# Row maxima and their scales on VectorE instead of TensorE for five of eight blocks, and input work spread over more steps

## The chip, the cores and the metric

The kernel runs on one core of one Trainium2 chip. The metric is the device time of one execution in microseconds (us), as the median of several executions; less is better. TensorE (PE in the profile) does the matrix products, its weight loads are listed as PEld. VectorE (DVE) and ScalarE (ACT) do the element-wise work, GpSimd (POOL) prepares weights early on, and the queue of SyncE (SP) issues the transfers.

## What is computed

```python
def act_quant(x):
    scale = 127.0 / jnp.clip(jnp.max(jnp.abs(x), axis=-1, keepdims=True), 1e-05, None)
    return jnp.clip(jnp.round(x * scale), -128.0, 127.0) / scale

scale = cond @ norm_w.T + 1.0
ms = jnp.mean(x * x, axis=-1, keepdims=True)
h = x * (scale[:, None, :] * jax.lax.rsqrt(ms + EPS))
u = h @ up_w.T
val, gate = jnp.split(u, 2, axis=-1)
h = val * jax.nn.gelu(gate, approximate=False)
hq = act_quant(h)                 # straight-through form left out
wq = weight_quant(down_w)         # to -1, 0, 1 times one scale
y = hq @ wq.T
return y + x
```

x is 4 x 1024 x 512 in float32, the hidden width is 2048, so up_w has 4096 rows. What matters here is act_quant: every token needs the largest absolute value of its 2048 hidden values before any of them can be rounded.

## The kernel before

The 4096 tokens are worked on in NB = 8 blocks of 512, numbered from 0 (the third block is b = 2). Within a block the hidden width is cut into J = 16 steps of 128, so that step n = 16 b + j makes hidden tile j of block b. A hidden tile has the 128 hidden values on the partitions and the 512 tokens along the free axis. Each float32 product is made of three float16 products (high and low parts of x and of the weights, names x_hi, x_lo, w_hi, w_lo). From block 2 on the value and gate products of a step are made of seven half-sized ones in place of eight (in_seven); for that the inputs of each block are first combined into sums and differences: difference on VectorE into ta, tb and xt, high on ScalarE (cast to x_hi), low on VectorE (the rest, x_lo). This is the "input work" of block b + 1, and it is done during block b, in steps 2, 3 and 15. It needs norm(b + 1, ...), four VectorE instructions in step 1.

There is no scheduler: each engine runs a program written out by hand, and semaphores hold it where it needs another. In a step n from block 2 on TensorE runs first_pair(n), third(n-1), gates(n-1), second(n), fourth(n-1), together 42 matmuls of 256 columns. ScalarE runs copies(n), absolute(n-2), gelu(n-1), and then the input work. VectorE runs hidden(n-2) (L1105), second_val(n-1) (L1093, waits for third), peak_of(n-2) (L1118, L1115 in step 0 of a block: the running maximum h_max over hidden tiles), residual (L1161), scaled (L1140: tiles of the block before are multiplied by their scale, which lies in ps_m), seed_gate(n) (L1088, waits for second(n) and is waited for by third(n)), rounded (L1147), then norm and the input work. From step 3 on two, one and one tiles of the block before are scaled and rounded per step, in turn (Q_COUNT), so steps 3, 6, 9 and 12 have two.

After these products TensorE has a tail in some steps. In steps 15, 0, 1 and 2 it is the second product, down, of an earlier block (16 matmuls of 512 columns, L674). The row maxima need TensorE too. h_max holds one maximum per partition and token; turn_max(b-1) at the end of step 1 of block b turns its four 128 x 128 parts by a transpose each (L657) into the PSUM bank ps_m. At the head of step 2 VectorE reduces ps_m along the free axis to one maximum per token (row_scales: L1122, L1125, L1127, L1129), with the tokens on the partitions. The scales are needed along the free axis again, equal on all partitions: spread_scale(b-1) in step 2 does that by four more transposes of a broadcast column (L663), ahead of down. norm reads ps_m as well, for the spread row factors of x, up to block 4; from block 5 on these come by a transfer. Once in blocks 3, 4 and 5, in step 11, VectorE runs rsqrt (L1031 to L1045), twelve small instructions. The last block's maxima are turned and spread after the loop.

Of the kernel before, what the change touches and what calls it, by code (L numbers as in the profile page):

```python
# [6 lines left out]
P = 128  # L7
ALU = mybir.AluOpType
ACT = mybir.ActivationFunctionType
F32 = mybir.dt.float32  # L10
# [32 lines left out]
def bass_cond_norm_geglu_bitlinear(  # L43
# [84 lines left out]

    def h_home(b, j):
        return J + j if j < 2 and b % 2 == 1 else j  # L130

    with ExitStack() as ctx:
# [48 lines left out]

        cond_sb = p5[:, 0, 0:B]
# [12 lines left out]
        row_max = sb("row_max", [P, TT], F32)  # L195
        row_rec = sb("row_rec", [P, TT], F32)
        row_scale = sb("row_scale", [P, TT], F32)
        dequant = sb("dequant", [P, 2, TT], F32)
        d_sums = sb("d_sums", [P, ND], F32)
# [82 lines left out]
        row_step = sem("row_step")  # L282
        scale_ready = sem("scale_ready")
# [9 lines left out]
        RS_STEPS = 11  # L293

# [68 lines left out]
        def _(sp):  # L363
# [111 lines left out]
            for n in range(NJ):  # L475
# [41 lines left out]
                if b == NB - 1 and j in (4, 5, 6):  # L517
                    if j == 4:
                        sp.wait_ge(x_lo_ready, made_before(NB))
                    load_late(2 * (j - 4))  # L520
                    load_late(2 * (j - 4) + 1)
# [16 lines left out]
        def _(pe):  # L538
# [121 lines left out]
            def spread_scale(b):  # L660
                pe.wait_ge(scale_ready, b + 1)
# [29 lines left out]
            for n in range(NJ + 1):  # L691
# [22 lines left out]
                if 1 <= b and j == 2:  # L714
                    spread_scale(b - 1)
# [43 lines left out]
        def _(act):  # L759
# [99 lines left out]
            for n in range(NJ + 2):  # L859
# [123 lines left out]
        def _(dve):  # L983
# [77 lines left out]
            def difference(c, k):  # L1061
                before = (c - 2) * 4
                if k == XT1:
                    dve.wait_ge(xn_ready, c * KT + 2)
                    dve.tensor_tensor(ta[:], xt[:, 0:2, HB:TB], xt[:, 0:2, 0:HB], ALU.subtract).then_inc(t_ready, 1)
                elif k == XT2:
                    dve.wait_ge(xn_ready, c * KT + 4)
                    dve.wait_ge(t_ready, before + 1)
                    dve.tensor_tensor(tb[:], xt[:, 2:4, HB:TB], ta[:], ALU.subtract).then_inc(t_ready, 1)
# [49 lines left out]

            def row_scales(b):  # L1120
                dve.wait_ge(max_rows, b + 1)
                dve.tensor_reduce(row_max[:], ps_m[:].rearrange("p (i n) -> p i n", i=TT), AX.X,  # L1122
                                  ALU.max).then_inc(row_step, 1)
                dve.wait_ge(row_step, 3 * b + 1)
                dve.tensor_scalar(row_max[:], row_max[:], CLIP, None, ALU.max).then_inc(row_step, 1)  # L1125
                dve.wait_ge(row_step, 3 * b + 2)
                dve.reciprocal(row_rec[:], row_max[:]).then_inc(row_step, 1)  # L1127
                dve.wait_ge(row_step, 3 * b + 3)
                dve.tensor_scalar(row_scale[:], row_rec[:], QMAX, None, ALU.mult).then_inc(scale_ready, 1)  # L1129

            def row_dequant(b):
                if b == 0:
                    dve.wait_ge(d_step, 5)
                dve.tensor_scalar(dequant[:, b % 2, :], row_max[:], 1.0 / QMAX, d_mean[:], ALU.mult,
                                  ALU.mult).then_inc(dequant_ready, 1)
# [14 lines left out]
            def residual(b, i, bank):  # L1150
# [3 lines left out]
                dve.wait_ge(dequant_ready, b + 1)  # L1154
# [39 lines left out]
            for n in range(NJ + 2):  # L1194
                b, j = divmod(n, J)
                if 1 <= b < NB and j == 2:
# [35 lines left out]
                if n < NJ and in_seven(n):  # L1232
                    seed_gate(n)
                for t in tiles:
# [96 lines left out]
```

## Time and profile before

| | us |
|---|---|
| median of 3 runs | 757.35 (757.11 to 757.44) |
| the profiled execution, device time | 756.66 |
| its span in the profile | 754.9 |
| TensorE busy (matmul) | 735.1, 97% |
| VectorE busy | 545.8, 72% |
| ScalarE busy | 348.7, 46% |
| GpSimd busy | 98.6, 13% |

The profile is of one execution; its span leaves out 1.8 us of the device time (756.66 less 754.9). Matmuls overlap in the rows: one has a duration, and the next starts before it ends, so that what a matmul costs its queue is the distance between two starts.

### The profile page before, as it was taken

The numbers are of one execution on the slowest core, as the hardware profiler recorded it, in microseconds if no ns is written. First come the engines' busy times: TensorE is split into PE (matmuls) and PEld (weight loads), VectorE is DVE, ScalarE is ACT, GpSimd is POOL, SyncE is SP. The second block draws the span as 40 slices with busy tenths as digits, with TensorE's granted clock in tenths as the row PEclk, the third lists the DMA queues.
The fourth block names the chain that finished last, engine by engine and source line by source line (L and its number), as shares of the span: only waits on it lengthen the run. The fifth ranks groups of instructions, "written<-read, shape, count | busy, mean of one in ns | idle before, by whom it ended". The sixth has DMA issues, their size and how long they took to land.

```text
span 754.9 us, 14213 instructions
## 1 busy us (share of the span) xinstructions
PE 735.1 (97%) x5462; PEld 536.5 (71%) x5462; DVE 545.8 (72%) x1066; ACT 348.7 (46%) x677; POOL 98.6 (13%) x137
## 2 busy tenths in 40 slices
PE   3999999999999999999999999999999999999998
PEld 2544444444677887888778887788778887688864
DVE  5467777888689775878667775777758776377747
ACT  5788866443164532553335543444425442243425
POOL 2211376763314000000000000000000000000000
PEclk9999999999999999999999999999999999999999
DMA  8777574756646454343533444343443333453302
GB/s 326 271 270 236 181 270 134 227 183 215 203 135 184 155 159 142 116 141 99 197 118 119 131 128 162 112 159 113 141 160 103 99 98 120 126 171 99 103 29 83
DMA packets 44787, 117.32 MB, mean 155 GB/s; under 512 B 5424, under 2 KB 5680, under 8 KB 43568
## 3 DMA queue, kind: packets, MB, share of 16 engines
q1 hardware_dynamic: 44720, 116.42, 47.8%
q8 instruction: 43, 0.70, 0.4%
q14 instruction: 24, 0.20, 0.1%
HBM read 99.62 MB, written 16.78 MB: 154 GB/s over the span
## 4 chain that ended last, share of the span: by engine, by line
PE 77%; DVE 12%; issue 5%; ACT 4%; DMA 1%; DVEq 0%; SPq 0%; POOL 0%; ACTq 0%
PE ps_v L552 13%; PE ps_v L553 13%; PE ps_v L554 13%; PE ps_y L674 12%; PE ps_g L553 5%; PE ps_g L552 5%; PE ps_g L554 5%; DVE h L1105 2%; DVE h L1140 2%; ACT g L781 2%; DVE h_max L1118 2%; PE ps_v L738 1%; PE ps_v L570 1%; PE ps_g L570 1%; PE ps_g L572 1%
## 5 line engine op out<-in xcount | busy, mean ns | idle before, releaser
L552 PE MATMUL ps_v<-x_hi,w_hi 128*128 128x256 f16 x968 | 264.5, 273 | 3.5 <-DVE ps_g L1088 1.3
L554 PE MATMUL ps_v<-x_hi,w_lo 128*128 128x256 f16 x968 | 264.4, 273 | 0.0
L553 PE MATMUL ps_v<-x_lo,w_hi 128*128 128x256 f16 x968 | 264.4, 273 | 0.0
L763 ACT COPY ps_g<-ps_v 128x256 f32<-128x256 f32 x96 | 34.3, 357 | 226.3 <-PE ps_v L554 226.3
L774 ACT ACTIVATE g<-ps_g,w_unscale 128x512 f32<-128x512 f32 x128 | 87.3, 682 | 67.8 <-PE ps_g L554 67.6
L1093 DVE TENSOR_TENSOR ps_v<-ps_v,p 128x256 f32<-128x256 f32 x96 | 41.4, 431 | 102.0 <-PE ps_v L554 102.0
L781 ACT ACTIVATE g<-h 128x512 f32<-128x512 f32 x128 | 81.3, 635 | 62.1 <-DVE h L1105 61.2
L1118 DVE TENSOR_TENSOR h_max<-g,h_max 128x512 f32<-128x512 f32 x120 | 84.9, 707 | 33.7 <-ACT g L781 25.6
L552 PEld LDWEIGHTS ps_v<-x_hi,w_hi 128*128 128x128 f16 x968 | 94.8, 98 | 19.3 <-DVE ps_g L1088 2.7
L552 PE MATMUL ps_g<-x_hi,w_hi 128*128 128x256 f16 x392 | 107.4, 274 | 0.0
L553 PE MATMUL ps_g<-x_lo,w_hi 128*128 128x256 f16 x392 | 107.4, 274 | 0.0
L554 PE MATMUL ps_g<-x_hi,w_lo 128*128 128x256 f16 x392 | 107.4, 274 | 0.0
L553 PEld LDWEIGHTS ps_v<-x_lo,w_hi 128*128 128x128 f16 x968 | 94.9, 98 | 13.1
L554 PEld LDWEIGHTS ps_v<-x_hi,w_lo 128*128 128x128 f16 x968 | 94.9, 98 | 11.1
L674 PE MATMUL ps_y<-dw,q 128*128 128x512 bf16 x448 | 101.3, 379 | 0.0
L1105 DVE SCALAR_TENSOR_TENSOR h<-ps_v,w_unscale,g 128x512 f32<-128x512 f32 x128 | 95.5, 746 | 2.4 <-PE ps_v L554 2.4
L1140 DVE TENSOR_TENSOR h<-h,ps_m 128x512 f32<-128x512 f32 x128 | 84.1, 680 | 1.8 <-PE ps_m L663 1.8
L674 PEld LDWEIGHTS ps_y<-dw,q 128*128 128x128 bf16 x448 | 43.8, 98 | 47.0
L1088 DVE TENSOR_TENSOR ps_g<-ps_v,p 128x256 f32<-128x256 f32 x96 | 41.3, 430 | 10.1 <-PE ps_v L554 4.3
L570 PE MATMUL ps_v<-x_hi,w_hi 128*128 128x512 f16 x124 | 47.0, 379 | 0.5 <-DVE h L1105 0.5
L1147 DVE TENSOR_SCALAR q<-h 128x512 bf16<-128x512 f32 x112 | 46.9, 440 | 0.3
L570 PE MATMUL ps_g<-x_hi,w_hi 128*128 128x512 f16 x124 | 47.0, 379 | 0.0
(127 smaller groups left out, 910.6 us busy)
## 6 DMA issues: line engine op xcount, KB each, us to landing
w_lo<-w_lo_dram SPq DMA_DIRECT2D x96, 448.0 KB, 3.3
q<-in_up_t_dram SPq DMA_DIRECT2D x16, 512.0 KB, 4.3
xt<-in_x_cols_dram SPq DMA_DIRECT2D x8, 1024.0 KB, 5.3
res<-in_x_rows_dram SPq DMA_DIRECT2D x26, 256.0 KB, 3.6
out_dram<-res SPq DMA_DIRECT2D x26, 256.0 KB, 2.7
sums<-in_up_t_dram SPq DMA_DIRECT2D x12, 512.0 KB, 4.5
xs<-in_x_rows_dram SPq DMA_DIRECT2D x22, 256.0 KB, 3.6
w_lo_dram<-w_lo SPq DMA_DIRECT2D x16, 256.0 KB, 4.3
```

Source lines behind the costliest of these rows:

```text
L552: pe.matmul(to, w_hi[:, wh:wh + P], hi, start=start and kt == 0, stop=False, skip_group_check=True)
L553: pe.matmul(to, w_hi[:, wh:wh + P], lo, start=False, stop=False, skip_group_check=True)
L554: last = pe.matmul(to, w_lo[:, wl:wl + P], hi, start=False, stop=(kt == 1), skip_group_check=True)
L570: pe.matmul(bank, w_hi[:, wh:wh + P], hi, start=start and kt == 0, stop=False)
L674: last = pe.matmul(ps_y[:, i % 2, :], q[:, j * TB + i * P:j * TB + (i + 1) * P], dw[:, j * D:(j + 1) * D], start=(j == 0), stop=(j == J - 1))
L774: act.activation(g[:, n % 3, :], ps_g[:, n % NG, :], ACT.Gelu, scale=w_unscale[:, n % J:n % J + 1]).then_inc(g_ready, 1)
L781: act.activation(g[:, n % 3, :], h[:, at:at + TB], ACT.Abs).then_inc(h_abs_ready, 1)
L1093: dve.tensor_tensor(ps_v[:, n % NV, HB:TB], ps_v[:, n % NV, 0:HB], p5[:, sevens(n) % 2, :], ALU.add).then_inc(v2_ready, 1)
L1105: dve.scalar_tensor_tensor(out=h[:, at:at + TB], in0=ps_v[:, n % NV, :], scalar=w_unscale[:, j:j + 1], in1=g[:, n % 3, :], op0=ALU.mult, o ...
L1118: dve.tensor_tensor(h_max[:], g[:, n % 3, :], h_max[:], ALU.max).then_inc(h_max_ready, 1)
L1140: dve.tensor_tensor(h[:, at:at + TB], h[:, at:at + TB], ps_m[:], ALU.mult).then_inc(scaled_ready, 1)
L1147: dve.tensor_scalar(to[:, j * TB:(j + 1) * TB], h[:, at:at + TB], ROUND, ROUND, ALU.add, ALU.subtract).then_inc(q_ready, 1)
```

## The change

For blocks 2 to 6 (by_vector) the two sets of transposes on TensorE are left out, and VectorE does both. turn_peaks, at the end of step 1 behind the four norm instructions, turns h_max in blocks of 32 x 32 by one transpose of 128 x 512 and reduces each run of 32, which leaves for every token four partial maxima in the four groups of 32 partitions. spread_peaks, in step 2 behind seed_gate, copies three groups to the partitions of the first, reduces the four, does the clip, reciprocal and factor on 32 x 16 elements, copies the result to the three other groups, and fills ps_m by a second transpose of 128 x 512 whose input is broadcast. row_scales is no longer run for these blocks. The one instruction for dequant becomes four on 32 partitions each. Where spread_scale is kept, it stands behind down in step 2 and no longer ahead of it (blocks 0 and 1; only block 1 has a down there). The two other input changes are for the inputs of blocks 4 to 7, made during blocks 3 to 6: of the six VectorE instructions of step 2 only the first difference stays there, two go to step 4, two to step 7 and one to step 10; of ScalarE's seven casts (four in step 2 and three in step 3) two stay in step 2, and one goes to step 5, one to 8, two to 9 and one to 11. New buffers are views of ta and tb; SyncE's late loads into them have one wait more.

```diff
+        turned = ta[:].rearrange("p a n -> p (a n)")
+        peak_rows = tb[:, 0, 0:TB // Q * TT].rearrange("p (k t) -> p k t", k=TT)
+        row_inv = tb[0:Q, 1, 0:TB // Q]
+        scale_all = tb[:, 1, TB // Q:2 * (TB // Q)]
...
+        row_peak = sb("row_peak", [P, TB // Q], F32)
...
+        def by_vector(b):
+            return V_FIRST <= b < NB - 1
...
+                        sp.wait_ge(scale_rows, NB - 1)
...
-                if 1 <= b and j == 2:
-                    spread_scale(b - 1)
                 for c in range(1, RS_DRAM):
                     if n == spread_rs_at(c):
                         spread_rs(c)
                 if b >= 2 and j < 3:
                     down(b - 2, j + 1)
+                if 1 <= b and j == 2 and not by_vector(b - 1):
+                    spread_scale(b - 1)
                 if b >= 1 and j == J - 1:
                     down(b - 1, 0)
-                if 1 <= b and j == 1:
+                if 1 <= b and j == 1 and not by_vector(b - 1):
                     turn_max(b - 1)
...
                         high(b + 1, XT1)
+                    if j == (2 if b < 3 else 5):
                         high(b + 1, XT2)
+                    if j == (2 if b < 3 else 8):
                         high(b + 1, XT3)
-                    if j == 3:
+                    if j == (3 if b < 3 else 9):
                         high(b + 1, XB21)
                         high(b + 1, XB22)
+                    if j == (3 if b < 3 else 11):
                         high(b + 1, XN4)
...
+                    if by_vector(c - 2):
+                        dve.wait_ge(peak_step, (c - 2 - V_FIRST) * PEAK_STEPS + 1)
...
+            def turn_peaks(b):
+
+                dve.wait_ge(h_max_ready, (b + 1) * J)
+                dve.wait_ge(x_hi_ready, made_before(b + 1))
+                dve.wait_ge(x_lo_ready, made_before(b + 1))
+                dve.transpose(turned, h_max[:]).then_inc(max_rows, 1)
+                dve.wait_ge(max_rows, b + 1)
+                dve.tensor_reduce(peak_rows[:, 0, :], turned.rearrange("p (t n) -> p t n", n=Q), AX.X,
+                                  ALU.max).then_inc(peak_step, 1)
+
+            def spread_peaks(b):
+
+                base = (b - V_FIRST) * PEAK_STEPS
+                dve.wait_ge(peak_step, base + 1)
+                for k in range(1, TT):
+                    dve.tensor_copy(peak_rows[0:Q, k, :], peak_rows[k * Q:(k + 1) * Q, 0, :]).then_inc(peak_step, 1)
+                dve.wait_ge(peak_step, base + 4)
+                dve.wait_ge(dequant_ready, dequants(b - 1))
+                dve.tensor_reduce(row_peak[0:Q, :], peak_rows[0:Q].rearrange("p k t -> p t k"), AX.X,
+                                  ALU.max).then_inc(peak_step, 1)
+                dve.wait_ge(peak_step, base + 5)
+                dve.tensor_scalar(row_peak[0:Q, :], row_peak[0:Q, :], CLIP, None, ALU.max).then_inc(peak_step, 1)
+                dve.wait_ge(peak_step, base + 6)
+                dve.reciprocal(row_inv, row_peak[0:Q, :]).then_inc(peak_step, 1)
+                dve.wait_ge(peak_step, base + 7)
+                dve.wait_ge(scale_rows, b)
+                dve.tensor_scalar(scale_all[0:Q, :], row_inv, QMAX, None, ALU.mult).then_inc(peak_step, 1)
+                dve.wait_ge(peak_step, base + 8)
+                for k in range(1, TT):
+                    dve.tensor_copy(scale_all[k * Q:(k + 1) * Q, :], scale_all[0:Q, :]).then_inc(peak_step, 1)
+                dve.wait_ge(peak_step, base + 11)
+                dve.wait_ge(xn_ready, min(b + 3, NB) * KT)
+                dve.wait_ge(scaled_ready, b * J)
+                dve.transpose(ps_m[:], scale_all.unsqueeze(2).to_broadcast([P, TB // Q, Q])).then_inc(scale_rows, 1)
...
+                else:
+                    for k in range(TT):
+                        dve.tensor_scalar(dequant[k * Q:(k + 1) * Q, b % 2, :],
+                                          row_peak[0:Q, :].rearrange("p (i k) -> p k i", k=TT)[:, k, :], 1.0 / QMAX,
+                                          d_mean[0:Q, :], ALU.mult, ALU.mult).then_inc(dequant_ready, 1)
...
-                if 1 <= b < NB and j == 2:
+                if 1 <= b < NB and j == 2 and not by_vector(b - 1):
                     row_scales(b - 1)
...
+                if 1 <= b < NB and j == 2 and by_vector(b - 1):
+                    spread_peaks(b - 1)
...
+                if 1 <= b < NB and j == 1 and by_vector(b - 1):
+                    turn_peaks(b - 1)
+                if 1 <= b < NB - 1:
                     if j == 2:
                         difference(b + 1, XT1)
+                    if j == (2 if b < 3 else 4):
                         difference(b + 1, XT2)
                         low(b + 1, XB11)
+                    if j == (2 if b < 3 else 7):
                         difference(b + 1, XT3)
                         low(b + 1, XT1)
+                    if j == (2 if b < 3 else 10):
                         difference(b + 1, XN4)
```

The new order is shown in block 3 at the turn from step 1 to 2, in step 2, and in step 4. The names are those of the section on the kernel; line numbers of the changed kernel differ.

TensorE, end of step 1 to the head of step 2, before:

```order
L554 MATMUL ps_v<-x_hi,w_lo 128x256
L674 MATMUL ps_y<-dw,q 128x512 x16
L657 MATMUL ps_m<-ident,h_max 128x128 x4
L552 MATMUL ps_v<-x_hi,w_hi 128x256
L553 MATMUL ps_v<-x_lo,w_hi 128x256
```

and after:

```order
L584 MATMUL ps_v<-x_hi,w_lo 128x256
L704 MATMUL ps_y<-dw,q 128x512 x16
L582 MATMUL ps_v<-x_hi,w_hi 128x256
L583 MATMUL ps_v<-x_lo,w_hi 128x256
L584 MATMUL ps_v<-x_hi,w_lo 128x256
```

The four transposes of h_max behind down are gone, and the products of step 2 follow at once.

TensorE, step 2, from its last product to step 3, before:

```order
L554 MATMUL ps_v<-x_hi,w_lo 128x256
L663 MATMUL ps_m<-ident,row_scale 128x128 x4
L674 MATMUL ps_y<-dw,q 128x512 x16
L552 MATMUL ps_v<-x_hi,w_hi 128x256
L553 MATMUL ps_v<-x_lo,w_hi 128x256
```

and after:

```order
L584 MATMUL ps_v<-x_hi,w_lo 128x256
L704 MATMUL ps_y<-dw,q 128x512 x16
L582 MATMUL ps_v<-x_hi,w_hi 128x256
L583 MATMUL ps_v<-x_lo,w_hi 128x256
L584 MATMUL ps_v<-x_hi,w_lo 128x256
```

The four transposes of row_scale ahead of down are gone too.

VectorE, end of step 1, from seed_gate on, before:

```order
L1088 TENSOR_TENSOR ps_g<-ps_v,p 128x256
L1058 SCALAR_TENSOR_TENSOR xt<-xt,cs,ps_m 128x512 x4
L1122 TENSOR_REDUCE row_max<-ps_m 128x4
L1125 TENSOR_SCALAR row_max<-row_max 128x4
L1127 RECIPROCAL row_rec<-row_max 128x4
L1129 TENSOR_SCALAR row_scale<-row_rec 128x4
L1105 SCALAR_TENSOR_TENSOR h<-ps_v,w_unscale,g 128x512
L1093 TENSOR_TENSOR ps_v<-ps_v,p 128x256
```

and after:

```order
L1125 TENSOR_TENSOR ps_g<-ps_v,p 128x256
L1091 SCALAR_TENSOR_TENSOR xt<-xt,cs,ps_m 128x512 x4
L1162 STREAM_TRANSPOSE ta<-h_max 128x512
L1164 TENSOR_REDUCE tb<-ta 128x16
L1142 SCALAR_TENSOR_TENSOR h<-ps_v,w_unscale,g 128x512
L1130 TENSOR_TENSOR ps_v<-ps_v,p 128x256
```

The reduction of ps_m and three small instructions ahead of hidden are replaced by a transpose and a reduction of SBUF data, with nothing of TensorE's between norm and them.

VectorE, step 2, from residual to hidden of step 3, before:

```order
L1161 SCALAR_TENSOR_TENSOR res<-ps_y,dequant,res 128x512
L1088 TENSOR_TENSOR ps_g<-ps_v,p 128x256
L1065 TENSOR_TENSOR ta<-xt 128x512
L1069 TENSOR_TENSOR tb<-xt,ta 128x512
L1083 TENSOR_TENSOR x_lo<-xt,x_hi 128x512
L1072 TENSOR_TENSOR xt<-xt 128x2x256
L1083 TENSOR_TENSOR x_lo<-ta,x_hi 128x512
L1077 TENSOR_TENSOR ta<-xt,tb 128x512
L1105 SCALAR_TENSOR_TENSOR h<-ps_v,w_unscale,g 128x512
```

and after:

```order
L1241 SCALAR_TENSOR_TENSOR res<-ps_y,dequant,res 128x512
L1125 TENSOR_TENSOR ps_g<-ps_v,p 128x256
L1172 COPY tb<-tb 32x16 x3
L1175 TENSOR_REDUCE row_peak<-tb 32x16
L1178 TENSOR_SCALAR row_peak<-row_peak 32x16
L1180 RECIPROCAL tb<-row_peak 32x16
L1183 TENSOR_SCALAR tb<-tb 32x16
L1186 COPY tb<-tb 32x16 x3
L1190 STREAM_TRANSPOSE ps_m<-tb 128x512
L1100 TENSOR_TENSOR ta<-xt 128x512
L1142 SCALAR_TENSOR_TENSOR h<-ps_v,w_unscale,g 128x512
```

Eleven instructions, with a transpose into ps_m as the last, stand where five of the six input instructions stood.

VectorE, step 4, before:

```order
L1118 TENSOR_TENSOR h_max<-g,h_max 128x512
L1140 TENSOR_TENSOR h<-h,ps_m 128x512
L1088 TENSOR_TENSOR ps_g<-ps_v,p 128x256
L1147 TENSOR_SCALAR q<-h 128x512
L1105 SCALAR_TENSOR_TENSOR h<-ps_v,w_unscale,g 128x512
L1093 TENSOR_TENSOR ps_v<-ps_v,p 128x256
```

and after:

```order
L1155 TENSOR_TENSOR h_max<-g,h_max 128x512
L1220 TENSOR_TENSOR h<-h,ps_m 128x512
L1125 TENSOR_TENSOR ps_g<-ps_v,p 128x256
L1227 TENSOR_SCALAR q<-h 128x512
L1106 TENSOR_TENSOR tb<-xt,ta 128x512
L1120 TENSOR_TENSOR x_lo<-xt,x_hi 128x512
L1142 SCALAR_TENSOR_TENSOR h<-ps_v,w_unscale,g 128x512
L1130 TENSOR_TENSOR ps_v<-ps_v,p 128x256
```

Two of the input instructions now stand at the end of this step; step 7 has two in the same place and step 10 one.

## Rows read from the trace of the kernel before

**Rows 1.** The page: busy us of the engines, and the granted clock in 40 slices

```profile
PE 735.1 (97%) x5462; PEld 536.5 (71%) x5462; DVE 545.8 (72%) x1066; ACT 348.7 (46%) x677; POOL 98.6 (13%) x137
...
PEclk9999999999999999999999999999999999999999
```

**Rows 2.** Busy time by stretch (one block): PE, PEld, DVE, ACT, POOL, clock, DMA

```profile
286.24:374.66 88.42, 88.22 (x747) 72.87 (x745) 64.41 (x133) 37.43 (x80) 0.00 (x0) 1.00 0.43 135
```

**Rows 3.** What TensorE waited for from 260 us on: total us, times, longest

```profile
PE ps_v L552 <- DVE ps_g L1088: 0.6, 3, 0.2
```

**Rows 4.** Timeline of TensorE, block 3, steps 1 to 3: start us, us

```profile
298.17 0.60 PE L657 MATMUL ps_m<-ident,h_max 128*128 128x128 f32 x4
298.61 0.27 PE L552 MATMUL ps_v<-x_hi,w_hi 128*128 128x256 f16 x1
...
303.19 0.60 PE L663 MATMUL ps_m<-ident,row_scale 128*128 128x128 f32 x4
303.63 3.62 PE L674 MATMUL ps_y<-dw,q 128*128 128x512 bf16 x16
```

**Rows 5.** The transposes of h_max over the whole run: ns min/median/max

```profile
L657 PE MATMUL ps_m<-ident,h_max x32: 272/273/273, 114.6 to 729.8; 128*128 128x128 f32 x32
```

**Rows 6.** Timeline of VectorE, block 3, steps 1 to 3: [idle before <-releaser]

```profile
294.61 2.71 DVE L1058 SCALAR_TENSOR_TENSOR xt<-xt,cs,ps_m 128x512 f32<-128x512 f32 x4
298.81 0.69 DVE L1122 TENSOR_REDUCE row_max<-ps_m 128x4 f32<-128x512 f32 x1 [1.49 <-PE ps_m L657]
...
299.74 0.18 DVE L1127 RECIPROCAL row_rec<-row_max 128x4 f32<-128x4 f32 x1
299.95 0.17 DVE L1129 TENSOR_SCALAR row_scale<-row_rec 128x4 f32<-128x4 f32 x1
300.06 0.75 DVE L1105 SCALAR_TENSOR_TENSOR h<-ps_v,w_unscale,g 128x512 f32<-128x512 f32 x1
300.77 0.43 DVE L1093 TENSOR_TENSOR ps_v<-ps_v,p 128x256 f32<-128x256 f32 x1
...
302.74 0.43 DVE L1088 TENSOR_TENSOR ps_g<-ps_v,p 128x256 f32<-128x256 f32 x1
303.08 0.68 DVE L1065 TENSOR_TENSOR ta<-xt 128x512 f32<-128x512 f32 x1
...
309.25 0.43 DVE L1093 TENSOR_TENSOR ps_v<-ps_v,p 128x256 f32<-128x256 f32 x1 [1.43 <-PE ps_v L554]
...
312.26 0.43 DVE L1088 TENSOR_TENSOR ps_g<-ps_v,p 128x256 f32<-128x256 f32 x1
```

**Rows 7.** Timeline of ScalarE, block 3, step 3

```profile
308.59 0.36 ACT L763 COPY ps_g<-ps_v 128x256 f32<-128x256 f32 x1 [2.18 <-PE ps_v L554]
...
309.12 0.64 ACT L781 ACTIVATE g<-h 128x512 f32<-128x512 f32 x1
```

**Rows 8.** Timeline of TensorE's weight loads: the first of third, step 3's seed

```profile
312.87 0.10 PEld L552 LDWEIGHTS ps_v<-x_hi,w_hi 128*128 128x128 f16 x1
```

**Rows 9.** Timeline of VectorE, block 3: second_val behind steps 4, 7 and 10

```profile
318.42 0.43 DVE L1093 TENSOR_TENSOR ps_v<-ps_v,p 128x256 f32<-128x256 f32 x1 [1.09 <-PE ps_v L554]
...
332.18 0.43 DVE L1093 TENSOR_TENSOR ps_v<-ps_v,p 128x256 f32<-128x256 f32 x1 [1.20 <-PE ps_v L554]
...
345.93 0.43 DVE L1093 TENSOR_TENSOR ps_v<-ps_v,p 128x256 f32<-128x256 f32 x1 [1.20 <-PE ps_v L554]
```

**Rows 10.** Timeline of VectorE, block 3, steps 11 and 12: rsqrt and after

```profile
348.57 0.16 DVE L1031 TENSOR_SCALAR ms<-sumsq 128x4 f32<-128x4 f32 x1
...
350.87 0.75 DVE L1105 SCALAR_TENSOR_TENSOR h<-ps_v,w_unscale,g 128x512 f32<-128x512 f32 x1
...
352.92 1.28 DVE L1140 TENSOR_TENSOR h<-h,ps_m 128x512 f32<-128x512 f32 x2
```

**Rows 11.** Timeline of TensorE at the same place

```profile
354.13 0.27 PE L554 MATMUL ps_v<-x_hi,w_lo 128*128 128x256 f16 x1
354.60 0.28 PE L552 MATMUL ps_v<-x_hi,w_hi 128*128 128x256 f16 x1 [0.20 <-DVE ps_g L1088]
```

More of the change, by code:

```diff
@@ L7 @@
 P = 128
+Q = 32
 ALU = mybir.AluOpType
@@ L127, in bass_cond_norm_geglu_bitlinear @@
     RS_DRAM = 5
+    V_FIRST = 2
     def h_home(b, j):
@@ L194, in bass_cond_norm_geglu_bitlinear @@
         rs_t = sb("rs_t", [P, TT], F32)
-        row_max = sb("row_max", [P, TT], F32)
-        row_rec = sb("row_rec", [P, TT], F32)
-        row_scale = sb("row_scale", [P, TT], F32)
         dequant = sb("dequant", [P, 2, TT], F32)
+        row_peak = sb("row_peak", [P, TB // Q], F32)
+        row_max = row_peak[:, 0:TT]
+        row_rec = row_peak[:, TT:2 * TT]
+        row_scale = row_peak[:, 2 * TT:3 * TT]
         d_sums = sb("d_sums", [P, ND], F32)
@@ L282, in bass_cond_norm_geglu_bitlinear @@
         row_step = sem("row_step")
+        peak_step = sem("peak_step")
         scale_ready = sem("scale_ready")
@@ L293, in bass_cond_norm_geglu_bitlinear, with scaled_before, dequants @@
         RS_STEPS = 11
+        PEAK_STEPS = 11
+        def by_vector(b):
+            return V_FIRST <= b < NB - 1
+        def scaled_before(b):
+            return sum(1 for k in range(b) if not by_vector(k))
+        def dequants(b):
+            return sum(TT if by_vector(k) else 1 for k in range(b + 1))
         def spread_rs_at(c):
@@ L660, in spread_scale @@
             def spread_scale(b):
-                pe.wait_ge(scale_ready, b + 1)
+                pe.wait_ge(scale_ready, scaled_before(b) + 1)
                 for i in range(TT):
@@ L1068, in difference @@
                     dve.wait_ge(t_ready, before + 1)
+                    if by_vector(c - 2):
+                        dve.wait_ge(scale_rows, c - 1)
                     dve.tensor_tensor(tb[:], xt[:, 2:4, HB:TB], ta[:], ALU.subtract).then_inc(t_ready, 1)
@@ L1120, in row_scales @@
             def row_scales(b):
+                base = 3 * scaled_before(b)
                 dve.wait_ge(max_rows, b + 1)
-                dve.tensor_reduce(row_max[:], ps_m[:].rearrange("p (i n) -> p i n", i=TT), AX.X,
+                dve.tensor_reduce(row_max, ps_m[:].rearrange("p (i n) -> p i n", i=TT), AX.X,
                                   ALU.max).then_inc(row_step, 1)
-                dve.wait_ge(row_step, 3 * b + 1)
-                dve.tensor_scalar(row_max[:], row_max[:], CLIP, None, ALU.max).then_inc(row_step, 1)
@@ L1126, in row_scales @@
[L1126 to L1129, printed above, removed]
+                dve.wait_ge(row_step, base + 1)
+                dve.tensor_scalar(row_max, row_max, CLIP, None, ALU.max).then_inc(row_step, 1)
+                dve.wait_ge(row_step, base + 2)
+                dve.reciprocal(row_rec, row_max).then_inc(row_step, 1)
@@ L1131, in row_dequant @@
+                dve.wait_ge(row_step, base + 3)
+                dve.tensor_scalar(row_scale, row_rec, QMAX, None, ALU.mult).then_inc(scale_ready, 1)
             def row_dequant(b):
@@ L1133, in row_dequant @@
                     dve.wait_ge(d_step, 5)
-                dve.tensor_scalar(dequant[:, b % 2, :], row_max[:], 1.0 / QMAX, d_mean[:], ALU.mult,
-                                  ALU.mult).then_inc(dequant_ready, 1)
+                if not by_vector(b):
+                    dve.tensor_scalar(dequant[:, b % 2, :], row_max, 1.0 / QMAX, d_mean[:], ALU.mult,
+                                      ALU.mult).then_inc(dequant_ready, 1)
+                else:
[3 more added lines that the diff above has]
+                                          d_mean[0:Q, :], ALU.mult, ALU.mult).then_inc(dequant_ready, 1)
             def scaled(b, j):
@@ L1153, in residual @@
                 dve.wait_ge(y_ready, u + 1)
-                dve.wait_ge(dequant_ready, b + 1)
+                dve.wait_ge(dequant_ready, dequants(b))
                 if late >= 0:
```

## The prediction

> **What bounds the kernel now.** I read the busy times of the page first: TensorE's matmuls cover 735.1 us of the span, VectorE has 545.8 us, and the granted clock stands at its top digit in all 40 slices, which is the 2.4 GHz level throughout [rows 1]. A busy share alone doesn't say that TensorE sets the end, since its durations overlap. So I read a stretch of one block's length next, 88.42 us from the first tail of block 3 on: 88.22 us of it are busy, at clock 1.00 [rows 2]. Then the waits: from 260 us to the end TensorE waits for another engine three times, for 0.6 us in all, always for seed_gate on VectorE [rows 3]. From there on each nanosecond that TensorE's queue has less to do shortens the run, as long as the other engines keep their appointments. The changed transposes all lie in this stretch (blocks 3 to 7, from about 298 us on).
>
> **Taken off TensorE.** The four transposes of h_max begin at 298.17 and the next product at 298.61, which is 0.44 us for four; the four of the scales begin at 303.19 and down at 303.63, 0.44 us again [rows 4]. Together 0.87 us per block, or 0.109 us for one. I take distances between starts and not the duration of 0.273 us [rows 5], since the next matmul starts 0.11 us after each in the same queue. Nothing of TensorE's waits stands beside them: the first product behind each follows without idle time. The change takes both sets out of five blocks (blocks 2 to 6, turned during blocks 3 to 7): 5 x 0.87 = 4.36 us. The last block and blocks 0 and 1 keep theirs. In block 2 spread_scale moves behind down; its reader is scaled in step 3, which waits for work behind the next first_pair anyway, and the sum of the queue is the same: 0.
>
> The Trainium skill (VectorE: DVE Perf Modes, "Rules for kernel authors") speaks against this change: it would have a 128 x 128 transpose on TensorE, and its page TensorE: Matmul & The Clock Gate (Part 4) puts one at some 275 ns within a kernel. As a duration the trace agrees (0.273 us), as a cost to the queue it doesn't (0.109 us); by the page's figure an estimate of what goes would be 40 x 0.275 = 11 us.
>
> **Added at the end of step 1, VectorE.** The four norms run from 294.61 to 297.32, then VectorE waits 1.49 us for the turned maxima and starts their reduction at 298.81 [rows 6]. Now a transpose of 128 x 512 and a reduction follow norm at once. No row shows a transpose on VectorE. Bounds: not less than the 0.43 us of an operation of half the elements (L1088), since 128 x 512 must be read; upward the trace gives no end, and I weigh that as a rival. I take 0.69 us, the duration of the other operations on 128 x 512 that read one tensor at one rate (L1122 in [rows 6]). Then the transpose starts at 297.3, the reduction at 297.9 or 298.0, and hidden at 298.7; hidden takes 0.7 us to the next start [rows 6]. second_val was at 300.77, set by TensorE; it is now due 0.44 us earlier, at 300.33. VectorE is there at 299.4, so 0.9 to 1.0 us are left: nothing on the path. The wait on TensorE's turn is gone and no other takes its place.
>
> **Added in step 2, VectorE.** seed_gate comes at 302.74 less 0.44 = 302.30, and spread_peaks 0.34 us behind it (303.08 less 302.74 [rows 6]), at 302.64. It has eleven instructions. A small one that waits for the one before takes 0.21 us from start to start (299.74 to 299.95), one that doesn't wait 0.11 us (299.95 to 300.06) [rows 6]. Six copies: 6 x 0.11 = 0.7 to 6 x 0.21 = 1.3 us. Reduction, clip, reciprocal and factor: 4 x 0.21, and up to 0.1 us more for 64 elements: 0.85 to 0.95 us. The transpose: 0.69 us, and up to 0.1 us for its three waits. Sum C: 2.2 to 3.0 us. I take 2.7, near the upper end, since copies into other partitions may not overlap.
>
> Who waits for that? Behind it stands the first difference (0.69 us), behind this ScalarE's cast of it, and in ScalarE's queue behind the cast copies(3), which TensorE needs. The cast can end no later than copies(3) is due: 308.59 [rows 7] less 0.87 = 307.72. With C it ends at 302.64 + C + 0.69 + 0.1 + 0.64 (the last from the other operation of its size in [rows 7]) = 304.07 + C = 306.8. So C may grow to 3.6 us and cost nothing. VectorE itself needs hidden(1) (0.7 us) before second_val, at 309.25 [rows 6] less 0.87 = 308.38, and would be ready for it at about 306.7. That step is the narrow one: seed_gate of step 3 ends at 312.69 (312.26 + 0.43 [rows 6]), and TensorE loads the first weights behind it at 312.87 [rows 8], 0.18 us later. But its chain starts with second_val, which TensorE releases (1.43 us of idle before it), and so it shifts with TensorE as a whole. The four instructions for dequant in step 5 cost up to 3 x 0.21 = 0.6 us more, behind which the idle time is like that behind step 4 (below): 0.
>
> **Moved input work.** The two instructions put into step 4 take 2 x 0.6 = 1.2 us from start to start (0.68 us long, overlapping by 0.08). second_val behind step 4 has 1.09 us of idle in front, those behind steps 7 and 10 have 1.20 us each [rows 9], and step 10 gets only one. So step 4 makes second_val 0.1 us late, step 7 not at all. The next operation, the running maximum, waits for ScalarE's absolute value of hidden, which now ends some 0.3 us later than before. seed_gate in a step with one tile can take this: with two tiles it takes 0.6 us more for scaled. There is a measure for it in the trace: rsqrt in step 11 adds 350.87 - 348.57 = 2.30 us in front of step 12, which has two tiles [rows 10]. The result is a gap of 354.60 - 354.13 = 0.47 us where 0.11 is usual, or 0.36 us [rows 11]. This is the wait of [rows 3], once each in blocks 3, 4 and 5. Half of that addition, in front of a step with one tile, gives none. And step 10's instruction is used up by the idle time before rsqrt, so the three stalls stay as they are: 0. ScalarE's casts: at most two in a step (1.2 us) at the end of its queue, where it stands idle for 2.18 us before copies(3) [rows 7], although step 2 now has four casts; in step 9 a square comes on top, for which I take 0.8 us (0.64 as in [rows 7] and the reading out of its sum), and copies(10) may be on the edge, 0 to 0.2 us in three blocks. I take 0. The casts and low parts are used in the next block only, and its five last ones stay in step 15. SyncE's new wait, for the scales of block 6, stands in step 4 of block 7 and is met in step 2: 0.
>
> **Sum.** -4.36 us on the profiled execution: span 754.9 to 750.5, device time 756.66 to 752.3. The median is 757.35, 0.7 us above the profiled one; 757.35 - 4.36 = **753.0 us**.
>
> **Rivals.**
>
> 1. *The transpose on VectorE is slow.* With a length x in place of 0.69, C = 2.0 + x, and the turn in step 1 has room up to x = 1.7. From x = 1.8 (C = 3.8, where the 0.18 us of step 3 are used up too) each further us costs about 2 us in each of the four blocks 3 to 6, once for each transpose. The 4.36 us are gone at x = 2.35 us (8 x 0.55). At four times 0.69, 2.75 us, the cost is 4 x 2 x 0.95 = 7.6 us, and the time 757.35 - 4.36 + 7.6 = 760.6. For it: no row shows the operation, and one that turns 32 x 32 values may go through them more than once. Against it: every operation on 128 x 512 in this trace takes 0.4 to 0.75 us. The Trainium skill (Vector Engine (DVE) Microarchitecture Reference, section 3.8) has it run at one element per cycle per lane, which would be an operation like the others; no run here shows it yet. 4 in 100.
>
> 2. *The moved input work meets the one- and two-tile rhythm.* If each of its three places costs what rsqrt costs, that is 3 x 4 x 0.36 = 4.3 us, and the time is 757.3: no change. Against it the idle time of [rows 9]. 4 in 100. A weaker form is likelier: one of the narrow places (seed_gate of step 3, the running maximum in step 5, copies(10)) costs 0.2 to 0.5 us per block, 1 to 2 us in all, 754 to 755. 9 in 100.
>
> 3. *The transposes cost TensorE their whole duration.* Then 40 x 0.273 = 10.9 us go, and the time is 746.4. That is also what the skill's figure above would give. Against it rows 4: four fit into 0.44 us. 1 in 100.
>
> 4. *The transposes are gone, but the time isn't.* TensorE's queue would have to hit a wait at once that these 0.87 us hid. VectorE is idle for 1.1 to 1.4 us before most of its appointments [rows 6, 9], and each follows TensorE's own work. 3 in 100, 756 to 757.5.
>
> **How the numbers follow.** The forecast, 752.4 to 753.8, has 79 in 100. The range goes from 752.2 (a little of the three stalls gone, and the scatter of 0.3 us between executions) to 754.6, into the weaker form of rival 2, so that 1 to 2 in 10 is outside. A change of 0.2% is 1.5 us, about what a measurement tells from none. Faster by more: forecast, weaker form and rival 3, less a little: 0.90. Within 0.2%: 0.06. Slower: rival 1 above x = 2.5, 0.04.
>
> **What the profile after would show.** Right: no transposes on TensorE between 290 and 700 us, a block of 87.55 us in place of 88.42 (88.42 - 0.87), both VectorE transposes at about 0.7 us, from seed_gate to the first difference 2.5 to 3.3 us, and TensorE's waits from 260 us on still three of 0.2 us. Wrong: a VectorE transpose above 1.8 us; new waits of TensorE for L1088's successor (L1125) in steps 4, 5, 6, 8 or 9, or for ScalarE's copies in steps 3 or 10; idle time of VectorE before the transposes.

## The result and the profile after

| kernel | median us (range) | ratio to the kernel before, 95% interval |
|---|---|---|
| before | 756.99 (756.76 to 757.44, 6 runs) | |
| changed | 752.35 (751.91 to 753.43, 6 runs) | 0.9941 (0.9931 to 0.9952) |

The change takes away 4.5 us (0.0059 x 757.0; by the interval 3.6 to 5.2). In a second comparison, with 5 runs, the changed kernel had 753.08 us and 0.9953 (0.9941 to 0.9966). The profiled execution took 751.99 us, its span is 750.2 us, against 756.66 and 754.9 before. One execution of e1 (below), the one of its first trace, ran at a granted clock of 0.95 and took 780.62 us; it is left out of every median and ratio here.

The page of the changed kernel, busy time and granted clock, to be held against [rows 1]:

```profile
PE 728.4 (97%) x5394; PEld 531.6 (71%) x5422; DVE 561.1 (75%) x1126; ACT 348.3 (46%) x677; POOL 100.0 (13%) x137
...
PEclk9999999999999999999999999999999999999999
```

TensorE has 5422 weight loads where it had 5462: the 40 transposes are gone. (Of the matmuls some records are missing, 28 by the same count, so the busy time says a little too much of a gain.) VectorE does 15.3 us more, and its share rises from 72% to 75%. The clock is unchanged.

What TensorE waited for from 260 us on, to be held against [rows 3], is word for word the same but for the line number:

```profile
PE ps_v L582 <- DVE ps_g L1125: 0.6, 3, 0.2
```

So no wait took the place of the transposes. The three stalls stand 87.54 us apart (353.44 and 440.98 for the first two) where they stood 88.42 us apart before (354.60 and 443.02): a block is 0.88 us shorter. VectorE's timeline in block 3, steps 1 to 3 (start us, us, [idle before <-releaser]), to be held against [rows 6]:

```profile
294.32 2.71 DVE L1091 SCALAR_TENSOR_TENSOR xt<-xt,cs,ps_m 128x512 f32<-128x512 f32 x4
296.95 0.70 DVE L1162 STREAM_TRANSPOSE ta<-h_max 128x512 f32<-128x512 f32 x1
297.69 0.69 DVE L1164 TENSOR_REDUCE tb<-ta 128x16 f32<-128x512 f32 x1
298.29 0.74 DVE L1142 SCALAR_TENSOR_TENSOR h<-ps_v,w_unscale,g 128x512 f32<-128x512 f32 x1
300.05 0.43 DVE L1130 TENSOR_TENSOR ps_v<-ps_v,p 128x256 f32<-128x256 f32 x1 [1.02 <-PE ps_v L584]
...
302.01 0.43 DVE L1125 TENSOR_TENSOR ps_g<-ps_v,p 128x256 f32<-128x256 f32 x1 [0.33 <-PE ps_v L584]
302.48 0.56 DVE L1172 COPY tb<-tb 32x16 f32<-32x16 f32 x3
303.07 0.25 DVE L1175 TENSOR_REDUCE row_peak<-tb 32x16 f32<-32x64 f32 x1
303.35 0.16 DVE L1178 TENSOR_SCALAR row_peak<-row_peak 32x16 f32<-32x16 f32 x1
303.55 0.24 DVE L1180 RECIPROCAL tb<-row_peak 32x16 f32<-32x16 f32 x1
303.82 0.16 DVE L1183 TENSOR_SCALAR tb<-tb 32x16 f32<-32x16 f32 x1
304.02 0.56 DVE L1186 COPY tb<-tb 32x16 f32<-32x16 f32 x3
304.61 0.73 DVE L1190 STREAM_TRANSPOSE ps_m<-tb 128x512 f32<-128x512 f32 x1
305.37 0.69 DVE L1100 TENSOR_TENSOR ta<-xt 128x512 f32<-128x512 f32 x1
305.98 0.74 DVE L1142 SCALAR_TENSOR_TENSOR h<-ps_v,w_unscale,g 128x512 f32<-128x512 f32 x1
308.09 0.43 DVE L1130 TENSOR_TENSOR ps_v<-ps_v,p 128x256 f32<-128x256 f32 x1 [1.36 <-PE ps_v L584]
```

The idle time of 1.49 us before the reduction is gone, and VectorE still waits for TensorE before both second_val: 1.02 and 1.36 us. The chain from the first copy to the first difference is 305.37 - 302.48 = 2.89 us. The two sets of transposes can be told apart here. With the 0.29 us added by which this trace is ahead before step 1 (294.32 for the norms' 294.61), second_val stands at 300.34 and 308.38, against 300.77 and 309.25 before: 0.43 us earlier behind the first set and 0.87 us behind both. ScalarE's cast behind it, and copies(3), to be held against [rows 7]:

```profile
306.10 0.62 ACT L846 CAST x_hi<-ta 128x512 f16<-128x512 f32 x1 [3.54 <-DVE ta L1100]
307.43 0.36 ACT L793 COPY ps_g<-ps_v 128x256 f32<-128x256 f32 x1 [0.72 <-PE ps_v L584]
```

**Where the time went.** A length that leaves out the start of the run goes from hidden of step 40 (block 2, step 8) to the last group of matmuls. Its two ends, of the kernel before and, from its own timelines, of the changed one:

```profile
252.21 0.74 DVE L1105 SCALAR_TENSOR_TENSOR h<-ps_v,w_unscale,g 128x512 f32<-128x512 f32 x1
...
750.27 1.04 PE L738 MATMUL ps_g<-dw,w_hi 128*128 128x256 bf16 x8
```

```profile
251.92 0.74 DVE L1142 SCALAR_TENSOR_TENSOR h<-ps_v,w_unscale,g 128x512 f32<-128x512 f32 x1
...
745.60 1.04 PE L768 MATMUL ps_g<-dw,w_hi 128*128 128x256 bf16 x8
```

498.06 us became 493.68: 4.38 us, where 4.36 were forecast. The other 0.29 us lie ahead of step 40, where other traces of the same work differ by more (below). I call this the late length. (Texts on record that speak of the last matmul count 0.77 us more, to the last of the group of eight.) The second trace of the changed kernel has 745.62 - 251.93 = 493.69 us. (Both profiled executions took 751.99 us, so this pair says nothing on the higher median of the second comparison.) Other traces show where executions differ: hidden of step 40 starts at 251.20 us in e4 and at 253.50 us in e5, whose work up to there is that of the changed kernel, at 251.92 us; and e4 and e2 have the late lengths of the changed kernel and of the kernel before to 0.03 and 0.01 us. So at least a good part of the scatter lies ahead of step 40, and the late length tells these kernels apart to a few hundredths.

### The profile page after: what moved, and what is told of

It is laid out like the page before. It is cut to its first block, busy times and chain, and to the rows that moved or that the text cites. A ratio compares the mean times of both kernels' runs of the same rounds, so it can differ in the third digit from the quotient of the medians.

```text
span 750.2 us, 14185 instructions
## 1 busy us (share of the span) xinstructions
PE 728.4 (97%) x5394; PEld 531.6 (71%) x5422; DVE 561.1 (75%) x1126; ACT 348.3 (46%) x677; POOL 100.0 (13%) x137
## 4 chain that ended last, share of the span: by engine, by line
PE 76%; DVE 13%; issue 5%; ACT 4%; DMA 0%; DVEq 0%; SPq 0%; POOL 0%; ACTq 0%
PE ps_v L582 13%; PE ps_v L584 13%; PE ps_v L583 13%; PE ps_y L704 12%; PE ps_g L584 5%; PE ps_g L583 5%; PE ps_g L582 5%; DVE h L1142 2%; DVE h L1220 2%; ACT g L811 2%; DVE h_max L1155 2%; PE ps_v L768 1%; PE ps_v L600 1%; PE ps_v L602 1%; PE ps_g L602 1%
## 5 line engine op out<-in xcount | busy, mean ns | idle before, releaser
L704 PE MATMUL ps_y<-dw,q 128*128 128x512 bf16 x422 | 96.1, 379 | 1.4
```

Source lines behind the costliest of these rows:

```text
L704: last = pe.matmul(ps_y[:, i % 2, :], q[:, j * TB + i * P:j * TB + (i + 1) * P], dw[:, j * D:(j + 1) * D], start=(j == 0), stop=(j == J - 1))
```

## The experiments

| kernel | median us | ratio (interval) | late length | against the changed kernel |
|---|---|---|---|---|
| e1: transposes only | 760.37 | 1.0047 (1.0031 to 1.0062) | | |
| e1 again | 759.96 | 1.0044 (1.0029 to 1.0059) | 501.44 | +7.76 |
| e2: input work only | 757.2 | 1.0006 (0.9997 to 1.0015) | 498.07 | +4.39 |
| e3: three blocks | 753.65 | 0.9961 (0.9948 to 0.9973) | 495.45 | +1.77 |
| e4: one transpose more | 752.79 | 0.9946 (0.9933 to 0.9960) | 493.71 | +0.03 |
| e5: three more | 758.42 | 1.0015 (1.0005 to 1.0024) | 498.99 | +5.31 |
| e6: rsqrt in step 10 | 752.03 | 0.9937 (0.9925 to 0.9950) | 492.58 | -1.10 |
| e7: input work of block 2 | 752.55 | 0.9944 (0.9931 to 0.9958) | 493.70 | +0.02 |
| e8: e6, e7, one block more | 751.79 | 0.9932 (0.9919 to 0.9944) | 492.58 | -1.10 |
| changed kernel again | 753.08 | 0.9953 (0.9941 to 0.9966) | 493.69 | +0.01 |
| e9: e6 and e7 | 750.56 | 0.9918 (0.9904 to 0.9931) | 492.59 | -1.09 |

Each ratio is against runs of the kernel before on the same chip.

### Halving the change: e2 and e1

e2 keeps the spread input work and turns nothing on VectorE:

```diff
-    V_FIRST = 2
+    V_FIRST = 8
```

> The changed kernel with V_FIRST = 8, so that TensorE turns the maxima and spreads the scales of all blocks; the input work stays spread over steps 2 to 11, and spread_scale stands behind down. My theory: this part moves work between idle times and gives nothing alone: 757.0 us, ratio to the kernel before 1.000 within 0.001, three stalls of TensorE of 0.36 us from 260 us on as before. Rival, that the spread input work brings part of the gain: 753 to 756.

Measured: 1.0006, and a late length of 498.07 us against 498.06 before. The input part alone gives nothing, to 0.01 us.

e1 keeps the transposes on VectorE and puts the input work back:

```diff
-                    if j == (2 if b < 3 else 4):
+                    if j == 2:
                         difference(b + 1, XT2)
                         low(b + 1, XB11)
...
```

(and so for the other steps, on ScalarE too)

> The changed kernel with the input work of blocks 4 to 7 put back into steps 2, 3 and 15. My theory: VectorE has room in step 2 for the new chain or for the six input instructions, not for both. In the changed kernel hidden(1) starts at 305.98 and second_val(2), due at 308.09, waits 1.36 us. Five input instructions more take 3.4 us from start to start, so hidden starts at 309.4, second_val some 2 us late, and ScalarE's third cast holds copies(3) until about 309.3 in place of 307.43. seed_gate of step 3 has 0.18 us of room, so TensorE loses about 1.7 us per block in the four blocks 3 to 6: 6.8 us, 759.2 us against 752.35 of the changed kernel, range 757 to 761, slower than the kernel before. Rival, that idle time of VectorE absorbs it since VectorE is busy for only 75% of the span: 752.4.

The kernel ran again, for a second trace:

> The kernel with the transposes on VectorE and the input work where it was, again, for a trace at the full granted clock. Its first trace had a clock of 0.95 and two waits of TensorE per block behind step 2, of 0.37 and 1.22 us. At the full clock I expect 1.6 to 2.0 us per block for blocks 3 to 6, so 500.8 to 502.4 us from hidden of step 40 to the last matmul (494.4 in the changed kernel), and 760 us in all.

Measured: 3.3 us slower than before (0.0044 x 756.7). VectorE, ScalarE and TensorE of the second trace, where step 2 ends and in step 3:

```profile
308.98 0.75 DVE L1142 SCALAR_TENSOR_TENSOR h<-ps_v,w_unscale,g 128x512 f32<-128x512 f32 x1
309.64 0.42 DVE L1130 TENSOR_TENSOR ps_v<-ps_v,p 128x256 f32<-128x256 f32 x1
```

```profile
307.70 0.62 ACT L846 CAST x_hi<-xt 128x512 f16<-128x512 f32 x1 [0.58 <-DVE xt L1109]
308.23 0.37 ACT L793 COPY ps_g<-ps_v 128x256 f32<-128x256 f32 x1
```

```profile
310.12 0.28 PE L582 MATMUL ps_v<-x_hi,w_hi 128*128 128x256 f16 x1 [0.34 <-DVE ps_v L1130]
...
313.37 0.28 PE L582 MATMUL ps_v<-x_hi,w_hi 128*128 128x256 f16 x1 [1.11 <-DVE ps_g L1125]
```

Neither second_val nor copies(3) has any idle time in front of it now; both are late, by 1.9 and 1.2 us (this trace is 0.38 us ahead of the changed kernel's before step 2; I had expected some 2 us and 1.9 us). TensorE's starts have three gaps per block beyond their usual distance, of 0.13, 0.51 and 1.27 us: 1.9 us, four times, is 7.6 of the 7.76 us. I had expected 1.7 us per block, and 1.6 to 2.0 us for the second trace. That VectorE stood idle for a quarter of the run helped nothing; its idle time is not where the work stands.

### How many blocks: e3

```diff
-    V_FIRST = 2
+    V_FIRST = 4
```

> The changed kernel with V_FIRST = 4: VectorE turns and spreads for blocks 4, 5 and 6 only, three blocks and not five. If the gain is the queue time of the transposes, it is 3 x 0.87 = 2.6 us: 754.4 us against 757.0 of before, ratio 0.9965. If it came from a wait that one block alone carries, it would be all (752.4) or much less (756 or more).

Measured: 0.9961, and a late length of 495.45, 2.61 us below the kernel before for three blocks, 0.87 us each. The full change has 4.38 for five, 0.88 each. The gain is proportional to the number of blocks, and so to the transposes taken away, at 0.109 us apiece.

### How much room the new chain has: e4 and e5

The second VectorE transpose is done twice (e4) or four times (e5):

```diff
+                dve.transpose(ps_m[:], scale_all.unsqueeze(2).to_broadcast([P, TB // Q, Q])).then_inc(peak_step, 1)
+                dve.wait_ge(peak_step, base + 12)
                 dve.transpose(ps_m[:], scale_all.unsqueeze(2).to_broadcast([P, TB // Q, Q])).then_inc(scale_rows, 1)
```

> The changed kernel with the second VectorE transpose (of the scales into ps_m) done twice in a row, waiting for each other: 0.76 us more in step 2 of each of the five blocks. My slack model: ScalarE's cast behind the chain ends at 306.72 and copies(3) starts at 307.43, so 0.7 us are free there, and 0.18 us more at seed_gate of step 3: 0 to 0.1 us per block, 752.4 to 752.9 us. Rival, that VectorE's chain is on the path: 5 x 0.76 = 3.8 us, 756.1.

> The changed kernel with the second VectorE transpose done four times, 2.3 us more in step 2 of each of five blocks. My slack model: 0.9 us are free (0.7 before ScalarE's copies(3), 0.18 at seed_gate of step 3), so 1.4 us are lost in each of the four blocks 3 to 6, and nothing in block 7, which has no input work: 5.6 us, 758.0 us, range 756.5 to 759.5. It is the test of the first rival of the prediction, a slow transpose. Rivals: all of it counts, 5 x 2.3 = 11.5 us, 763.9; none does, 752.4.

e4 costs 0.03 us for 0.76 us more in each of five blocks: the chain is off the path. In its trace ScalarE's cast ends where copies(3) starts, the 0.72 us of above are used up:

```profile
306.14 0.62 ACT L846 CAST x_hi<-ta 128x512 f16<-128x512 f32 x1 [4.30 <-DVE ta L1100]
306.71 0.36 ACT L793 COPY ps_g<-ps_v 128x256 f32<-128x256 f32 x1
```

e5 costs 5.31 us. Its waits of TensorE from 260 us on, and its timeline in step 3 of block 3:

```profile
PE ps_v L582 <- DVE ps_g L1125: 3.2, 7, 0.7
PE ps_v L582 <- ACT p L796: 1.0, 4, 0.3
```

```profile
311.19 0.28 PE L582 MATMUL ps_v<-x_hi,w_hi 128*128 128x256 f16 x1 [0.26 <-ACT p L796]
314.65 0.28 PE L582 MATMUL ps_v<-x_hi,w_hi 128*128 128x256 f16 x1 [0.66 <-DVE ps_g L1125]
```

TensorE waits for ScalarE's copies four times, once in each of blocks 3 to 6, and for seed_gate seven times, of which three are the old ones. Both are the places that the prediction named. The gaps are 0.42 and 0.82 us per block, 1.24 us where 1.4 were expected, so about 1.0 us of the 2.3 was free, where 0.9 was expected. A gap of 0.23 us in block 7 is one that I had not expected. From this the break-even can be estimated. e5 ends 0.93 us above the late length of the kernel before, which is 0.23 us in each of four blocks, so a chain some 2.05 us longer (2.28 less 0.23) would give all of the gain back. e5 lengthens only the transpose of step 2; the other half of the first rival, a slow transpose in step 1, was not run.

### The three stalls that stayed: e6

```diff
-            return {1: 5, 2: 14, 3: J + 12, 4: 2 * J + 15}.get(c, (c - 2) * J + 11)
+            return {1: 5, 2: 14, 3: J + 12, 4: 2 * J + 15}.get(c, (c - 2) * J + 10)
...
-                    if j == (2 if b < 3 else 10):
+                    if j == (2 if b < 3 else 13):
                         difference(b + 1, XN4)
```

(the cast of the last difference from step 11 to 14)

> The changed kernel with rsqrt of blocks 5, 6 and 7 in step 10 and not in step 11, and the last difference and its cast moved from steps 10 and 11 to 13 and 14. If TensorE's three stalls of 0.36 us from 260 us on come from rsqrt's 2.3 us directly ahead of a step with two tiles, a single-tile step between them takes them away: 3 x 0.36 = 1.1 us less than the changed kernel, 751.3 us, ratio to the kernel before 0.9926. Rival, that the stall only moves: 752.4.

Measured: the late length falls by 1.10 us, and the trace has no wait of TensorE after 260 us. VectorE in the step between rsqrt and the step with two tiles:

```profile
346.24 0.75 DVE L1142 SCALAR_TENSOR_TENSOR h<-ps_v,w_unscale,g 128x512 f32<-128x512 f32 x1
...
350.48 0.43 DVE L1130 TENSOR_TENSOR ps_v<-ps_v,p 128x256 f32<-128x256 f32 x1 [0.16 <-PE ps_v L584]
351.03 0.69 DVE L1155 TENSOR_TENSOR h_max<-g,h_max 128x512 f32<-128x512 f32 x1
351.64 1.28 DVE L1220 TENSOR_TENSOR h<-h,ps_m 128x512 f32<-128x512 f32 x2
```

With one tile in step 11 VectorE has caught up (0.16 us of idle time) before step 12's two tiles. Of the two edits it is rsqrt's that counts: the last difference stood in step 2 in the kernel before, which had the same three stalls. The medians alone (752.03 against 752.35) would not have shown it.

### Block 2: e7, e8 and e9

e7 moves the input work made during block 2 behind that block's weight work:

```diff
-                    if j == (2 if b < 3 else 4):
+                    if j == (2 if b < 2 else 10 if b == 2 else 4):
                         difference(b + 1, XT2)
                         low(b + 1, XB11)
...
```

> The changed kernel with the input work made during block 2 moved too: two instructions to step 10, two to step 11, one to step 13, behind the weight work of steps 2 to 8. In the changed kernel TensorE stands still at 221.81 (0.81 us), 224.66 (0.22), 233.97 (0.11), 236.56 (0.61) and 240.55 (1.36). The first two follow on the five input instructions of step 2 and should go: 1.0 us less, 751.3 us; the three others follow on weight work in steps 5, 6 and 8 and may stay. Rival, that the weight work alone makes all five: 752.4.

The gap of 0.81 us fell to 0.17 (at 222.38 in its trace), that of 0.22 stayed at 0.23, the three others too. The median didn't show it: this trace had a gap of 1.29 us at 178.79, where the changed kernel has 0.72, in a stretch that the edit doesn't touch. By the median alone e7 is inconclusive. The gap of 0.81 us is not the same in every execution, either: it is 0.45 us in the traces of e3 and e4, whose program there is that of the changed kernel. The last section shows what makes the difference, and that e7's edit takes some 0.7 us of the gap away in like conditions.

> The last two changes together, and V_FIRST = 1, so that VectorE turns and spreads for block 1 too (during block 2, whose step 2 has no input work but the first difference now). If each holds: 752.4 - 1.1 - 1.0 - 0.87 = 749.4 us, ratio 0.990. Rival, that spread_peaks and the weight work in step 2 of block 2 don't fit together: 750 to 751.5.

e8 misses the 749.4 us and comes near the rival's time. Where TensorE waited between 215 and 250 us, of the changed kernel and then of e8:

```profile
PE ps_v L582 <- DVE ps_v L1130: 1.2, 1, 1.2
PE ps_v L582 <- DVE ps_g L1125: 1.1, 2, 0.6
```

```profile
PE ps_v L582 <- DVE ps_v L1130: 2.7, 2, 1.6
PE ps_v L582 <- DVE ps_g L1125: 0.4, 1, 0.4
```

The eight transposes less of block 1 (0.87 us) and the smaller gap at 222 us (0.6 us) are paid back: 1.0 us of it by a new wait for second_val (a gap of 1.23 us at 224.25 where the changed kernel has 0.23) and 0.4 us by a longer one at 240.69 (1.75 for 1.36). The time is near the rival's, but the rival's reason, that the chain and the weight work don't fit into step 2, is not what the trace shows. VectorE does both and still waits for TensorE before second_val; it is late only one step further on, where rounded and the weight instruction take 1.29 and 1.74 us in place of the changed kernel's 0.75 and 1.27, while GpSimd works. VectorE of e8 in steps 2 and 3, then GpSimd:

```profile
213.02 0.73 DVE L1190 STREAM_TRANSPOSE ps_m<-tb 128x512 f32<-128x512 f32 x1
213.78 1.28 DVE L1051 SCALAR_TENSOR_TENSOR xs<-sums,w_scale,w_hi 128x1024 f16<-128x1024 f32 x1
...
216.50 0.43 DVE L1130 TENSOR_TENSOR ps_v<-ps_v,p 128x256 f32<-128x256 f32 x1 [0.17 <-PE ps_v L584]
...
220.24 1.29 DVE L1227 TENSOR_SCALAR q<-h 128x512 bf16<-128x512 f32 x2
221.45 1.74 DVE L1051 SCALAR_TENSOR_TENSOR xs<-sums,w_scale,w_hi 128x1024 f16<-128x1024 f32 x1
```

```profile
220.23 1.01 POOL L964 TENSOR_TENSOR sums<-sums 128x256 f32<-128x256 f32 x1
221.32 0.79 POOL L966 TENSOR_TENSOR sums<-sums 128x256 f32<-128x256 f32 x1
```

The excess of the two, 0.54 and 0.47 us, is the 1.0 us of the new wait. Whether every execution of e8 meets GpSimd in this way one trace doesn't say, so it stays open whether six blocks on VectorE could be better than five. e9 leaves block 1 on TensorE:

> rsqrt in step 10, and the input work of block 2 behind its weight work, but TensorE still turns for block 1. From the traces: 1.1 us less than the changed kernel from block 3 on (493.3 us from hidden of step 40 to the last matmul), and 0.65 us less in step 3 of block 2: 1.7 us less than the run beside it, about 750.7 us. Rival, that the stalls in block 2 grow elsewhere by what is taken away, as in the kernel that also turned block 1 on VectorE: 1.1 us less, 751.3.

Measured beside the changed kernel: 750.56 us and 0.9918 against 753.08 and 0.9953, intervals apart. That is 2.5 us less where 1.7 was expected, of which 1.1 are in the late length and some 0.7 to 0.8 in the gap at 222; the rest, some 0.6 us, is not placed and lies within the scatter between executions. It has the lowest median of this study; the interval of e8's ratio overlaps with its own, so the two are not told apart.

## Why the prediction was right

**The bound and the sum.** 753.0 us (752.2 to 754.6) were forecast and 752.35 measured. The median alone proves little: it lies 0.15 us inside the range and 0.05 us below the band of 752.4 to 753.8 that was to have 79 in 100, single executions went from 751.91 to 753.43, and the second comparison gave 753.08. The 753.0 were also counted from 757.35 us, where six executions of the kernel before have 756.99; the fall itself is 4.5 us by the ratio. What carries the prediction is the term. The sum was one term, 40 transposes at 0.109 us by distances between starts, and e3 and the late lengths confirm the term and its proportion: 4.38 us for 4.36, and a block of 87.54 us for 87.55. The third rival, by the duration of 0.273 us, is out by a factor of 2.5.

**The terms of zero.** These were the real risk. The turn in step 1: 0.70 us for a forecast of 0.69, idle time 1.02 us behind it for 0.9 to 1.0. The chain in step 2: 2.89 us for a forecast of 2.7 (2.2 to 3.0); the six copies take 0.20 us each from start to start although only two of them wait for another's result, so the upper bound was the right one. The chain also began 0.47 us behind seed_gate (302.48 less 302.01), not 0.34, so that from seed_gate to the first difference it took 3.36 us, a little outside the 2.5 to 3.3 us that the prediction had named as its sign. The cast ended 0.7 us before copies(3), where C = 2.7 had left 0.9. The input work: second_val behind step 4 has no idle time left and comes 0.03 us late (0.1 forecast), and the running maximum behind it 0.26 us later (some 0.3 forecast); copies(10) kept 0.28 us of idle time, and e2 shows the cost of all of it as 0.01 us. The four dequant instructions of step 5 were taken too low: they take 1.00 us from the first to hidden, where the single one took 0.13, so 0.87 us more for a forecast of up to 0.6. They cost nothing, but the idle time before the next second_val fell from 1.07 to 0.16 us: this term came nearer to the path than the prediction has it. The three stalls stayed, as forecast.

**The rivals.** The slow transpose: 0.70 and 0.73 us rule it out, and e5, which makes it true artificially for the transpose of step 2, costs what its model said, within 0.2 us per block. The weaker form of the second rival, 1 to 2 us, had 9 in 100 and did not come. What the prediction did not tell is how the two halves hang together: the first half alone is slower than before (e1), the second gives nothing (e2), and their sum gives all. The prediction had costed each edit in the presence of the other.

## What to carry to other kernels

Where one engine's queue has no gaps, an instruction moved off it gives back the distance between its start and the next one's, not its duration (here 0.109 us, not 0.273). Whether the gain is kept is decided by the appointments of the engine that takes the work: list, for each wait of the full queue, how long its releaser stood idle before, and add the new work up to the narrowest. Where that overflows, first move other work out of that step, even if this gives nothing by itself.

## What the runs showed of the hardware

A VectorE transpose of 128 x 512 float32 takes 0.70 us to SBUF and 0.73 us to PSUM from a broadcast input. The Trainium skill (Vector Engine (DVE) Microarchitecture Reference, section 3.8) has the transpose keep up one element per cycle per lane. The trace agrees in so far as it takes as long as the other operations of 128 x 512 that read one tensor (0.69 us). Copies of 32 x 16 between groups of partitions start 0.20 us apart without a wait between them, while a small instruction on 128 partitions let the next one start after 0.11 us [rows 6].

In block 2 some VectorE instructions took far longer than usual while GpSimd worked. In the changed kernel's trace the running maximum behind second_val of step 2 took 1.05 us in place of 0.69, and GpSimd's instruction after it 1.06 in place of 0.73:

```profile
218.50 1.05 DVE L1155 TENSOR_TENSOR h_max<-g,h_max 128x512 f32<-128x512 f32 x1 [0.36 <-ACT g L811]
```

```profile
218.28 0.73 POOL L962 TENSOR_TENSOR sums<-sums 128x256 f32<-128x256 f32 x1
219.09 1.06 POOL L964 TENSOR_TENSOR sums<-sums 128x256 f32<-128x256 f32 x1
```

In e4, whose program up to there is the same, VectorE was first by 0.02 us, and only GpSimd's instruction is long:

```profile
218.22 0.69 DVE L1155 TENSOR_TENSOR h_max<-g,h_max 128x512 f32<-128x512 f32 x1 [0.36 <-ACT g L811]
```

```profile
218.24 1.26 POOL L962 TENSOR_TENSOR sums<-sums 128x256 f32<-128x256 f32 x1
```

Nine traces have the same VectorE work in this step (all but e7, e8, e9 and the first of e1). In three (before, e3, e4) the maximum starts just before GpSimd's instruction and takes 0.69 us. In the six others it starts while one of GpSimd's is running and takes 1.05 to 1.25 us, and each time it ends 0.55 us after that one does: what starts second waits for what runs. TensorE's gap at 222 us follows exactly. It is the maximum's time less 0.24 us in all nine, from 0.45 to 1.01 us. In e7 and e9, with the input work gone from step 2, the maximum took 1.09 and 1.01 us and the gap is 0.17 and 0.09 us, 0.7 us less than by this rule. So this meeting costs TensorE up to 0.56 us per execution, a part of the scatter ahead of step 40 (2.3 us from e4 to e5). When GpSimd starts depends on its wait for a transfer, and no run moved that.
